# A threshold search over half the chip's counting work: VectorE compares without a running sum and TensorE adds the pieces

## The chip, the cores and the metric

The kernel runs on one core of one Trainium2 chip. The metric is the device time of one execution in microseconds (us), smaller is better. The core has five engines that run side by side and meet only at semaphores: TensorE (PE in the profile, with its weight loads as PEld), VectorE (DVE), ScalarE (ACT), GpSimd (POOL) and SyncE (SP), which issues the transfers.

## What is computed

Two hybrid layers over x of shape (2, 512, 512): attention, gated feed-forward and a state-space scan in the first, grouped attention, LoRA experts and a sparse gated feed-forward in the second. The change touches only the sparse one (`_L1_attn_b_ref`), which zeroes, in every row, the half of the 1376 gate values that is smallest in magnitude:

```python
s = jax.nn.silu(jnp.einsum('bsh,ih->bsi', x, w_gate))
B, S, I = s.shape                       # I = 1376
k = int(K_FACTOR * I)                   # 688
_, idx = jax.lax.top_k(-jnp.abs(s), k)
flat = flat.at[rows, idx.reshape(B * S, k)].set(0.0)
s = s * jnp.einsum('bsh,ih->bsi', x, w_up)
return jnp.einsum('bsi,hi->bsh', s, w_down)
```

## The kernel before

Each batch b (0 and 1) has 512 rows, held as four tiles t of 128 rows; so |s| is eight tiles `k_abs[b][t]` of 128 partitions x 1376 floats. The order of the stages is a list made by `schedule()`; each engine walks it in program order. The stage of interest is `("topk", 1)`, near the end. Before it stand the gate projections, behind it two normalisations and two LoRA stages.

The threshold of each row is found by a search over the 31 bits of a positive float (`K_BITS`). In step n each batch has a candidate per row (`k_cand`, integer bits, read as a float). For every row the number of values under the candidate is counted; from the count the bit is kept or cleared and the next one set. The counting is shared out by `K_DVE = [1, 2]`:

- VectorE (`count_low`, L1798) takes tile 0 of batch 0 and tiles 0 and 1 of batch 1: one instruction compares 1376 values with the row's candidate and also sums the ones into `k_cnt` (`accum_out`).
- ScalarE (L1367) takes the other five tiles: a Sign activation of candidate minus value, summed into `k_diff`.

`update(b, n)` on VectorE turns counts into the next candidate: L1805 (VectorE's tiles), L1807 (ScalarE's tiles, behind the semaphore `count[b]`), L1808 (the new bits, which signals `cand[b]`, for which both engines wait before they count that batch again). The order on VectorE is written out by hand, per step n: `count_low(0, n)`, `update(1, n-1)`, `count_low(1, n)`, `multiply_up(n-2)` in 24 of the 31 steps, `update(0, n)`. So the update of one batch lies behind a compare of the other. ScalarE alternates: batch 0's tiles, then batch 1's.

`multiply_up` (L1816) multiplies one result of the "up" projection, from a PSUM bank, into `k_s`. There are 24 such results: three column groups (512, 512, 352 wide) times eight row tiles; TensorE makes each with 12 matmuls (`mm3` is three matmuls: low x high, high x low, high x high). In the kernel before TensorE makes them at the start of the stage as fast as PSUM banks come free, one bank for each row tile, eight in all. The weights of the projection are units that SP loads and GpSimd splits into a high and a low part (L583, L584), in a ring of eight; a unit is split when TensorE has released the one eight before it.

After the search `threshold(b)` counts once more, on VectorE with L1827, the tiles that ScalarE had (three of batch 0, two of batch 1), adjusts their thresholds, and eight `mask` steps follow, then the down projection.

Of the kernel before, what the change touches and what calls it, by code (L numbers as in the profile page):

```python
# [49 lines left out]
K_DVE = [1, 2]  # L50
# [187 lines left out]
k_bits k_cand_0 k_cand_1 k_less_0 k_less_1 k_count_0 k_count_1 k_thr k_diff k_mask k_gate k_up k_silu k_up_kept k_abs k_masked k_turned k_hi k_lo k_acc  # L238
# [16 lines left out]
def hybrid_layers(nc, x_d, units_d, const_d, small_d, bdown_d, out_d):  # L255
# [9 lines left out]
    with ExitStack() as ctx:  # L265
        def sb(name, shape, dt=F32):
            return ctx.enter_context(nc.sbuf_tensor(name, shape, dt))
# [7 lines left out]
        cand, less, count = ([s[f"k_{n}_{b}"] for b in range(B)] for n in ("cand", "less", "count"))  # L275
# [8 lines left out]
        ra_lo = sb("ra_lo", [P, HC * EW], F32R)  # L284
        negA = sb("negA", [P, DT * N_ST])
# [9 lines left out]
        sd = sb("sd", [P, TT])  # L295
        f_hi = sb("f_hi", [P, 2, 512], F32R)
        f_lo = sb("f_lo", [P, 2, 512], F32R)
# [75 lines left out]
        k_junk = k_eq.bitcast(BF16).rearrange("p (a c) -> p a c", a=2)  # L373
        k_sign = k_rank.bitcast(BF16).rearrange("p (a c) -> p a c", a=2)
# [249 lines left out]
        def _(pe):  # L624
# [40 lines left out]
            def release(k=1):  # L665
                at["u"] += k
                at["owed"] += k
# [382 lines left out]
            def topk(_):  # L1050
                for j, w in enumerate(TK_W):
                    for b in range(B):
                        for t in range(TT):
                            rows(claim(b * TT + t, s["k_up_kept"]), [("tu", j, k) for k in range(HC)], hT_hi[:, b], hT_lo[:, b], t, w, s["k_up"], b)
# [341 lines left out]
        def _(dve):  # L1396
# [392 lines left out]
            def topk(_):  # L1789

                def count_low(b, n):

                    dve.wait_ge(cand[b], n + 1)
                    for t in range(K_DVE[b]):
                        last = before(n, b, t, 2)
                        if last:
                            dve.wait_ge(less[last[0]], last[1])
# [12 lines left out]

                def multiply_up(n):

                    j, b, t = n // (B * TT), n // TT % B, n % TT
                    y = k_s[b][t][:, 512 * j:512 * j + TK_W[j]]
                    need(s["k_up"])
                    go(V.tensor_tensor(y, ps[:, b * TT + t, 0:TK_W[j]], y, ALU.mult), s["k_up_kept"])  # L1816

                def threshold(b):
# [3 lines left out]
                    k_low, k_high, k_up = (k_late[:, n, 0:TT - m] for n in range(3))  # L1822
                    dve.wait_ge(cand[b], K_BITS + 1)
                    for r in range(B):
                        dve.wait_ge(less[r], K_DVE[r] * K_BITS)
# [3 lines left out]
                    go(V.tensor_scalar(k_low, late, 0xFFFF, None, ALU.bitwise_and))  # L1829
                    did(V.tensor_scalar(k_high, late, 16, None, ALU.logical_shift_right))  # L1830
                    did(V.tensor_tensor(k_low, k_low, k_up, ALU.add))
                    did(V.tensor_scalar(k_up, k_low, 16, None, ALU.logical_shift_right))
                    go(V.tensor_scalar(k_low, k_low, 0xFFFF, None, ALU.bitwise_and))
                    did(V.tensor_tensor(k_high, k_high, k_up, ALU.add))
                    did(V.tensor_scalar(k_high, k_high, 16, None, ALU.logical_shift_left))
                    did(V.tensor_tensor(late, k_high, k_low, ALU.bitwise_or), s["k_thr"])
# [35 lines left out]
                before = counted(lambda b: range(K_DVE[b]))  # L1872
# [129 lines left out]
```

## Time and profile before

| | us |
|---|---|
| median of 3 runs | 2974.18 |
| lowest and highest run | 2952.24 and 2975.89 |
| the profiled execution, its own time | 2963.2 |
| its span, first to last instruction | 2961.4 |
| busy: TensorE / VectorE / ScalarE / GpSimd | 2392.7 / 2051.9 / 1586.4 / 1214.4 |
| TensorE's granted clock, mean of the span | 0.898 of full speed |

The profile is of one execution. The busy times are sums over stages with different limits, so none of them says what bounds the threshold search; that has to be read from the stretch in which it runs, the last eighth of the span or so.

### The profile page before, as it was taken

The numbers are of one execution on the slowest core, as the hardware profiler recorded it, in microseconds if no ns is written. First come the engines' busy times: TensorE is split into PE (matmuls) and PEld (weight loads), VectorE is DVE, ScalarE is ACT, GpSimd is POOL, SyncE is SP. The second block draws the span as 40 slices with busy tenths as digits, with TensorE's granted clock in tenths as the row PEclk, the third lists the DMA queues.
The fourth block names the chain that finished last, engine by engine and source line by source line (L and its number), as shares of the span: only waits on it lengthen the run. The fifth ranks groups of instructions, "written<-read, shape, count | busy, mean of one in ns | idle before, by whom it ended". The sixth has DMA issues, their size and how long they took to land.

```text
span 2961.4 us, 36619 instructions
## 1 busy us (share of the span) xinstructions
PE 2392.7 (81%) x12216; PEld 1868.2 (63%) x12216; DVE 2051.9 (69%) x3145; ACT 1586.4 (54%) x3315; POOL 1214.4 (41%) x1016
## 2 busy tenths in 40 slices
PE   6986989858888848878899799998799998951068
PEld 4344347657777647777777588876688877741056
DVE  3743743668899657989753678874778874598984
ACT  2551641267876237787411466663566663799611
POOL 3022036253334422244465556673556663510081
PEclk9797799979999968999999899999999999965578
DMA  6224213020101120020123111121111121200011
GB/s 215 44 77 117 44 53 90 25 79 19 61 26 29 43 79 15 11 72 26 40 89 89 40 47 45 53 58 47 43 43 54 43 61 46 83 15 0 0 43 36
DMA packets 87842, 155.73 MB, mean 53 GB/s; under 512 B 8840, under 2 KB 17672, under 8 KB 87528
## 3 DMA queue, kind: packets, MB, share of 16 engines
q1 hardware_dynamic: 87656, 153.38, 17.6%
q8 instruction: 100, 1.64, 0.2%
q14 instruction: 86, 0.70, 0.1%
HBM read 138.21 MB, written 14.75 MB: 52 GB/s over the span
## 4 chain that ended last, share of the span: by engine, by line
PE 46%; DVE 18%; ACT 15%; issue 8%; POOL 3%; DVEq 0%; ACTq 0%; POOLq 0%
PE ps L640 40%; ACT tables L1367 5%; PE ps L654 5%; DVE m L1580 2%; DVE m L1606 2%; DVE f_lo L1406 2%; ACT m L1231 2%; DVE m_front L1527 1%; PE ps L779 1%; POOL w_lo L584 1%; ACT m L1210 1%; DVE f_hi L1405 1%; DVE loose L1509 1%; ACT L1231 1%; ACT tables L1200 1%
## 5 line engine op out<-in xcount | busy, mean ns | idle before, releaser
L583 POOL TENSOR_SCALAR w_hi<-w_in 128x512 fp32r<-128x512 f32 x430 | 352.0, 819 | 1219.5 <-PE ps L640 663.9
L584 POOL TENSOR_TENSOR w_lo<-w_in,w_hi 128x512 fp32r<-128x512 f32 x430 | 648.0, 1507 | 35.9
L640 PE MATMUL ps<-hT_hi,w_lo 128*128 128x512 f32 x864 | 364.0, 421 | 29.4 <-DVE a L1451 12.7
L640 PE MATMUL ps<-hT_lo,w_hi 128*128 128x512 f32 x864 | 346.1, 401 | 0.0
L640 PE MATMUL ps<-hT_hi,w_hi 128*128 128x512 f32 x864 | 345.6, 400 | 0.0
L1606 DVE TENSOR_TENSOR_SCAN m<-m,m 128x1028 f32<-128x1028 f32 x128 | 315.1, 2462 | 10.3 <-ACT m L1231 3.1
L640 PEld LDWEIGHTS ps<-m,tables 128*128 128x128 f32 x2048 | 253.3, 196 | 53.6 <-ACT tables L1200 25.6
L640 PE MATMUL ps<-m,tables 128*128 128x128 f32 x2048 | 258.3, 280 | 32.7 <-ACT tables L1200 32.6
L654 PE MATMUL ps<-tables,m 128*128 128x128 f32 x1024 | 144.3, 284 | 100.2 <-DVE m L1606 72.2
L1231 ACT ACTIVATE m<-m_rows,negA 128x256 f32<-128x256 f32 x512 | 217.7, 504 | 0.4
L1200 ACT ACTIVATE tables<-ps 128x512 f32<-128x512 f32 x256 | 139.1, 593 | 142.9 <-PE ps L654 142.9
L640 PEld LDWEIGHTS ps<-hT_hi,w_lo 128*128 128x128 f32 x864 | 168.5, 195 | 65.5 <-DVE a L1451 16.1
L640 PE MATMUL ps<-g,g 128*128 128x128 f32 (+3 forms) x704 | 173.2, 394 | 38.4 <-ACT g L1292 15.2
L640 PEld LDWEIGHTS ps<-hT_hi,w_hi 128*128 128x128 f32 x864 | 167.7, 194 | 38.4
L1580 DVE TENSOR_TENSOR m<-m,m 128x1024 f32<-128x1024 f32 x128 | 187.4, 1464 | 5.9 <-ACT m L1192 3.9
L654 PEld LDWEIGHTS ps<-tables,m 128*128 128x128 f32 x1024 | 117.8, 145 | 116.0 <-issue 84.7
L640 PEld LDWEIGHTS ps<-hT_lo,w_hi 128*128 128x128 f32 x864 | 168.8, 195 | 29.9
L640 PEld LDWEIGHTS ps<-g,g 128*128 128x128 f32 x704 | 121.2, 192 | 100.3 <-issue 61.5
L640 PE MATMUL ps<-w_hi,g 128*128 128x512 f32 x512 | 177.3, 407 | 7.5 <-DVE x_sb L1409 4.7
L1479 DVE TENSOR_REDUCE a<-ps 128x2 f32<-128x1024 f32 x128 | 150.1, 1221 | 44.7 <-PE ps L640 44.3
L1133 ACT ACTIVATE a<-ps 128x512 f32<-128x512 f32 x256 | 138.9, 595 | 72.6 <-PE ps L640 72.2
L640 PE MATMUL ps<-a,a 48*128 48x512 f32 (+1 forms) x512 | 147.7, 529 | 30.9 <-ACT a L1133 17.8
(247 smaller groups left out, 5314.0 us busy)
## 6 DMA issues: line engine op xcount, KB each, us to landing
w_in<-units SPq DMA_DIRECT2D x430, 256.0 KB, 2.6
stack_scratch<-a SPq DMA_DIRECT2D x48, 256.0 KB
a<-stack_scratch SPq DMA_DIRECT2D x64, 192.0 KB, 4.5
m<-bc_scratch SPq DMA_DIRECT2D x16, 512.0 KB, 5.4
out<-x_sb SPq DMA_DIRECT2D x2, 1024.0 KB, 4.3
tables<-small SPq DMA_DIRECT2D x1, 1143.0 KB, 10.3
x_sb<-x SPq DMA_DIRECT2D x4, 256.0 KB, 3.5
x_sb<-x SPq DMA_DIRECT2D x1, 1024.0 KB, 7.9
```

The lines of the kernel that those rows point to most:

```text
L583: c["did"](nc.gpsimd.tensor_scalar(w_hi[:, r], raw, 1.0, 1.0, ALU.mult, ALU.mult), s["unit_hi"])
L584: c["did"](nc.gpsimd.tensor_tensor(w_lo[:, r], raw, w_hi[:, r].bitcast(F32), ALU.subtract), s["unit_split"])
L640: ins = T.matmul(out, lhsT, rhs, start=start, stop=stop)
L654: ins = T.transpose(out, in_, ident)
L1133: go(A(a_pT[:, kT % 2 * 4 + pair * 2 + h], ps[:, 4 + h], ACT.Exp, scale=A_DK ** -0.5), s["a_exp"])
L1200: go(A(m_hT[:, part], ps[:, 6 - part], ACT.Copy), s["m_hT_kept"])
L1231: go(A(m_dA[:, n % DA_RING * NG + r, 1:SEG], m_dt[:, tile % 4], ACT.Exp, scale=negA[:, st:st + 1]), s["m_dA"])
L1367: A(k_sign[:, done % 2], k_abs[b][t], ACT.Sign, bias=k_cand[:, b].bitcast(F32)[:, t:t + 1], scale=-1.0, accum_out=k_diff[:, b, t:t + 1]).t ...
L1406: did(V.tensor_tensor(lo, src, hi.bitcast(F32), ALU.subtract), sem)
L1479: go(V.reduce_max(top, ps[:, pair * 2:pair * 2 + 2], AX.X), s["a_max"])
L1580: go(V.tensor_tensor(m_st[:, slot:slot + NG, 1:SEG], m_dtx[:, i % 2].unsqueeze(1).broadcast_to([P, NG, HL]), m_bc[:, g * NG:(g + 1) * NG], ...
L1606: V.tensor_tensor_scan(states, m_dA[:, dA:dA + NG].rearrange("p a t -> p (a t)"), states, 0.0, ALU.mult, ALU.add)\
```

## The change

`K_DVE` becomes `[2, 2]`: VectorE has four tiles and ScalarE four. VectorE's compare has no `accum_out` any more: it writes 0.5 or -0.5 per value (is-less, then minus 0.5) in bf16 into buffers of its own, `k_low[b][t]`. TensorE then adds eight pieces of 172 columns of each such tile onto one another, in PSUM, by multiplying with a bf16 identity matrix (`k_ident`): 8 matmuls per tile, 32 per step. VectorE's update begins with a reduction over the remaining 172 columns of both tiles (128x344 in PSUM, two sums out), behind a new semaphore `total[b]`, and then has one comparison for all four tiles in place of two.

TensorE's order is now written out: per step `sums(0, n)`, the first half (6 matmuls) of up result n, `sums(1, n)`, its second half. The up results go round six PSUM banks (`K_BANKS`); banks 6 and 7 take the sums. `threshold(b)` has two tiles to count for each batch.

```diff
-K_DVE = [1, 2]
+K_DVE = [2, 2]
+K_CHUNK = INTER // 8
+K_BANKS = 6
 ...
+                def sums(b, n):
+                    o = claim(K_BANKS + b, summed[b])
+                    if b == n == 0:
+                        need(s["k_ident_set"])
+                    for t in range(K_DVE[b]):
+                        pe.wait_ge(less[b], K_DVE[b] * n + t + 1)
+                        for r in range(INTER // K_CHUNK):
+                            ins = T.matmul(o[:, t * K_CHUNK:(t + 1) * K_CHUNK], k_ident, k_low[b][t][:, r * K_CHUNK:(r + 1) * K_CHUNK],
+                                           start=r == 0, stop=(r + 1) * K_CHUNK == INTER)
+                    ins.then_inc(total[b], 1)
+
+                for n in range(K_BITS):
                     for b in range(B):
-                        for t in range(TT):
-                            rows(claim(b * TT + t, s["k_up_kept"]), ...)
-                    release(HC)
+                        sums(b, n)
+                        if n < B * TT * len(TK_W):
+                            up(n, b)
 ...
                     for t in range(K_DVE[b]):
-                        V.tensor_scalar(k_junk[:, (n + b + t) % 2], k_abs[b][t], k_cand[:, b].bitcast(F32)[:, t:t + 1], None, ALU.is_lt, ALU.add,
-                                        accum_out=k_cnt[:, b, t:t + 1]).then_inc(less[b], 1)
+                        V.tensor_scalar(k_low[b][t], k_abs[b][t], k_cand[:, b].bitcast(F32)[:, t:t + 1], 0.5, ALU.is_lt, ALU.subtract)\
+                            .then_inc(less[b], 1)
 
                 def update(b, n):
                     bit, m = float(1 << K_BITS - 1 - n), K_DVE[b]
-                    dve.wait_ge(less[b], m * (n + 1))
-                    go(V.tensor_scalar(k_no[:, b, 0:m], k_cnt[:, b, 0:m], TOPK - 0.5, bit, ALU.is_ge, ALU.mult))
+                    dve.wait_ge(total[b], n + 1)
+                    did(V.tensor_reduce(k_diff[:, b, 0:m], ps[:, K_BANKS + b, 0:m * K_CHUNK].rearrange("p (t c) -> p t c", t=m), AX.X, ALU.add), summed[b])
                     dve.wait_ge(count[b], (TT - m) * (n + 1))
-                    did(V.tensor_scalar(k_no[:, b, m:], k_diff[:, b, m:], 2.0 * TOPK - INTER - 0.5, bit, ALU.is_ge, ALU.mult))
+                    did(V.tensor_scalar(k_no[:, b], k_diff[:, b], -0.5, bit, ALU.is_ge, ALU.mult))
                     V.scalar_tensor_tensor(k_cand[:, b], k_cand[:, b], k_bit[:, n + 1:n + 2], k_no[:, b], ALU.bitwise_or, ALU.bitwise_xor)\
                         .then_inc(cand[b], 1)
```

`up(n, part)`, not shown, is the old `rows` for one result cut in two at its inner loop.

## Rows read from the trace of the kernel before

**Rows 1.** Windows view of the search: length, busy and count per engine, clock, DMA.
```profile
2553.00:2775.00 222.00, 86.15 (x284) 68.56 (x283) 198.68 (x398) 221.18 (x311) 22.85 (x24) 0.63 0.05 16
```
**Rows 2.** Chain of work that ended last, same stretch, by line.
```profile
by line: ACT tables L1367 65.8%; issue 33.0%; DVE tables L1827 1.5%; DVE k_rows L1808 0.1%; DVE k_rows L1807 0.1%; DVE k_rows L1871 0.0%; ACTq L1362 0.0%
```
**Rows 3.** ScalarE's count of one tile, all 31 steps: ns min/median/max, first and last start.
```profile
L1367 ACT ACTIVATE tables<-loose,k_rows x31: 1424/1426/1429, 2559.1 to 2773.0; 128x1376 bf16<-128x1376 f32 x31
```
**Rows 4.** Timeline of VectorE inside the search: start us, us, instruction, idle before.
```profile
2671.21 0.69 DVE L1816 TENSOR_TENSOR k<-ps,k 128x512 f32<-128x512 f32 x1
2671.81 0.14 DVE L1805 TENSOR_SCALAR k_rows<-k_rows 128x1 int32<-128x1 f32 x1
...
2674.74 0.17 DVE L1807 TENSOR_SCALAR k_rows<-k_rows 128x2 int32<-128x2 f32 x1 [0.65 <-ACT tables L1367]
2674.95 0.22 DVE L1808 SCALAR_TENSOR_TENSOR k_rows<-k_rows,k_rows,k_rows 128x4 int32<-128x4 int32 x1
2675.20 1.65 DVE L1798 TENSOR_SCALAR_CACHE_REDUCE tables<-k,k_rows 128x1376 bf16<-128x1376 f32 x1
...
2676.78 1.64 DVE L1798 TENSOR_SCALAR_CACHE_REDUCE tables<-k,k_rows 128x1376 bf16<-128x1376 f32 x1
...
2685.47 0.52 DVE L1816 TENSOR_TENSOR k<-ps,k 128x352 f32<-128x352 f32 x1
2685.91 0.14 DVE L1805 TENSOR_SCALAR k_rows<-k_rows 128x1 int32<-128x1 f32 x1
```
**Rows 5.** Single lines of VectorE, whole run: ns min/median/max, starts, forms.
```profile
L1798 DVE TENSOR_SCALAR_CACHE_REDUCE tables<-k,k_rows x93: 1640/1645/1649, 2553.3 to 2769.4; 128x1376 bf16<-128x1376 f32 x93
L1550 DVE TENSOR_SCALAR tables<-m_rows x16: 427/430/1387, 611.0 to 1383.5; 128x512 f32<-128x512 f32 x16
L1466 DVE TENSOR_SCALAR negA<-negA x1: 228/228/228, 72.4 to 72.4; 128x128 f32<-128x128 f32 x1
L1429 DVE TENSOR_SCALAR n<-x_sb,mv,sd x64: 536/545/1543, 8.5 to 2933.6; 128x512 f32<-128x512 f32 x64
L1669 DVE TENSOR_REDUCE g<-ps x192: 424/558/683, 1664.8 to 2447.4; 128x1 f32<-128x256 f32 x64, 128x1 f32<-128x384 f32 x64, 128x1 f32<-128x512 f32 x64
```
**Rows 6.** Timeline of VectorE: four L1429, GpSimd idle, and four, GpSimd working.
```profile
2921.79 1.92 DVE L1429 TENSOR_SCALAR n<-x_sb,mv,sd 128x512 f32<-128x512 f32 x4
8.51 4.10 DVE L1429 TENSOR_SCALAR n<-x_sb,mv,sd 128x512 f32<-128x512 f32 x4
```
**Rows 7.** The new candidate's instruction, as in rows 5.
```profile
L1808 DVE SCALAR_TENSOR_TENSOR k_rows<-k_rows,k_rows,k_rows x62: 221/223/1323, 2559.3 to 2779.0; 128x4 int32<-128x4 int32 x62
```
**Rows 8.** Timeline of TensorE: 512, 128 and 136 moving columns at full clock.
```profile
1201.36 2.05 PE L640 MATMUL ps<-m,tables 128*128 128x128 f32 x16 [0.88 <-ACT tables L1200]
...
2559.18 0.39 PE L640 MATMUL ps<-w_hi,hT_hi 128*128 128x512 f32 x1
2559.41 0.39 PE L640 MATMUL ps<-w_hi,hT_lo 128*128 128x512 f32 x1
...
2927.35 0.42 PE L640 MATMUL ps<-ra_lo,hT_hi 128*128 128x136 f32 x1
2927.57 0.41 PE L640 MATMUL ps<-ra_hi,hT_hi 128*128 128x136 f32 x1
```
**Rows 9.** Page, costliest groups: busy us, mean ns of one, idle before, releaser.
```profile
L640 PE MATMUL ps<-m,tables 128*128 128x128 f32 x2048 | 258.3, 280 | 32.7 <-ACT tables L1200 32.6
```
**Rows 10.** Windows view, columns as in rows 1: a dense stretch, and two of the search.
```profile
1200.00:1240.00 40.00, 35.77 (x255) 31.95 (x254) 37.36 (x30) 33.81 (x77) 10.28 (x7) 1.00 0.00 1
2581.00:2630.00 49.00, 31.64 (x85) 22.03 (x84) 44.72 (x93) 49.00 (x69) 1.40 (x2) 0.75 0.04 11
2644.00:2686.00 42.00, 23.33 (x72) 20.61 (x72) 37.90 (x80) 42.00 (x60) 0.00 (x0) 0.50 0.00 0
```
**Rows 11.** Chain behind the search, in order of time: start us, us, line.
```profile
2772.11 1.67 DVE tables L1827 x2
2773.80 1.67 DVE tables L1827 x2
```

More of the change, by code:

```diff
@@ L274, in hybrid_layers @@
         max_in = [s["a_max_in_0"], s["a_max_in_1"]]
-        cand, less, count = ([s[f"k_{n}_{b}"] for b in range(B)] for n in ("cand", "less", "count"))
+        cand, less, count, total, summed = ([s[f"k_{n}_{b}"] for b in range(B)] for n in ("cand", "less", "count", "sum", "summed"))
         stack_out = [s["a_stack_out_0"], s["a_stack_out_1"]]
@@ L284, in hybrid_layers @@
         ra_lo = sb("ra_lo", [P, HC * EW], F32R)
+        negA_at = nc.sbuf_base
         negA = sb("negA", [P, DT * N_ST])
@@ L295, in hybrid_layers @@
         sd = sb("sd", [P, TT])
+        f_at = [nc.sbuf_base]
         f_hi = sb("f_hi", [P, 2, 512], F32R)
+        f_at.append(nc.sbuf_base)
         f_lo = sb("f_lo", [P, 2, 512], F32R)
@@ L373, in hybrid_layers @@
         k_junk = k_eq.bitcast(BF16).rearrange("p (a c) -> p a c", a=2)
+        k_ident = nc.alloc_sbuf_tensor_at("k_ident", [P, P], BF16, offset=negA_at, align_bytes=4)[:, :]
+        k_low = [[k_junk[:, 0], k_junk[:, 1]]]
+        k_low.append([nc.alloc_sbuf_tensor_at(f"k_low_{n}", [P, INTER], BF16, offset=base, align_bytes=4)[:, :] for n, base in enumerate(f_at)])
         k_sign = k_rank.bitcast(BF16).rearrange("p (a c) -> p a c", a=2)
@@ L1050, in topk, with up @@
             def topk(_):
-                for j, w in enumerate(TK_W):
+                def up(n, part):
+                    j, b, t = n // (B * TT), n // TT % B, n % TT
+                    o = claim(n % K_BANKS, s["k_up_kept"]) if part == 0 else ps[:, n % K_BANKS]
+                    w, rows_w = TK_W[j], slice(t * P, (t + 1) * P)
+                    for k in range(2 * part, 2 * part + 2):
+                        hi, lo = unit(("tu", j, k), k)
+                        mm3(o[:, 0:w], hT_hi[:, b, k, rows_w], hT_lo[:, b, k, rows_w], hi[:, 0:w], lo[:, 0:w],
+                            k == 0, k == HC - 1, s["k_up"] if k == HC - 1 else None)
+                    if part and n % (B * TT) == B * TT - 1:
+                        release(HC)
+                def sums(b, n):
[9 more added lines that the diff above has]
+                for n in range(K_BITS):
                     for b in range(B):
-                        for t in range(TT):
-                            rows(claim(b * TT + t, s["k_up_kept"]), [("tu", j, k) for k in range(HC)], hT_hi[:, b], hT_lo[:, b], t, w, s["k_up"], b)
-                    release(HC)
+                        sums(b, n)
+                        if n < B * TT * len(TK_W):
+                            up(n, b)
                 for b in range(B):
@@ L1815, in multiply_up @@
                     need(s["k_up"])
-                    go(V.tensor_tensor(y, ps[:, b * TT + t, 0:TK_W[j]], y, ALU.mult), s["k_up_kept"])
+                    go(V.tensor_tensor(y, ps[:, n % K_BANKS, 0:TK_W[j]], y, ALU.mult), s["k_up_kept"])
                 def threshold(b):
@@ L1821, in threshold @@
                     late, thr = c_b[:, m:], c_b.bitcast(F32)
-                    k_low, k_high, k_up = (k_late[:, n, 0:TT - m] for n in range(3))
+                    k_lower, k_high, k_up = (k_late[:, n, 0:TT - m] for n in range(3))
                     dve.wait_ge(cand[b], K_BITS + 1)
-                    for r in range(B):
-                        dve.wait_ge(less[r], K_DVE[r] * K_BITS)
                     for t in range(m, TT):
@@ L1828, in threshold @@
                     did(V.tensor_scalar(k_up, k_cnt[:, b, m:], TOPK - 0.5, None, ALU.is_lt))
-                    go(V.tensor_scalar(k_low, late, 0xFFFF, None, ALU.bitwise_and))
+                    go(V.tensor_scalar(k_lower, late, 0xFFFF, None, ALU.bitwise_and))
                     did(V.tensor_scalar(k_high, late, 16, None, ALU.logical_shift_right))
-                    did(V.tensor_tensor(k_low, k_low, k_up, ALU.add))
-                    did(V.tensor_scalar(k_up, k_low, 16, None, ALU.logical_shift_right))
-                    go(V.tensor_scalar(k_low, k_low, 0xFFFF, None, ALU.bitwise_and))
+                    did(V.tensor_tensor(k_lower, k_lower, k_up, ALU.add))
+                    did(V.tensor_scalar(k_up, k_lower, 16, None, ALU.logical_shift_right))
+                    go(V.tensor_scalar(k_lower, k_lower, 0xFFFF, None, ALU.bitwise_and))
                     did(V.tensor_tensor(k_high, k_high, k_up, ALU.add))
                     did(V.tensor_scalar(k_high, k_high, 16, None, ALU.logical_shift_left))
-                    did(V.tensor_tensor(late, k_high, k_low, ALU.bitwise_or), s["k_thr"])
+                    did(V.tensor_tensor(late, k_high, k_lower, ALU.bitwise_or), s["k_thr"])
                 def mask(b, t):
@@ L1871, in topk @@
                     V.memset(k_cand[:, b], 1 << K_BITS - 1).then_inc(cand[b], 1)
-                before = counted(lambda b: range(K_DVE[b]))
+                assert 2 * TOPK == INTER
+                go(V.tensor_copy(k_ident, ident), s["k_ident_set"])
                 for n in range(K_BITS):
```

5 lines of the change are left out of this document (1 added, 4 removed).

## The prediction, made before the changed kernel ran

> **What bounds the kernel now.** I read the page first: TensorE is busiest over the span, which says nothing of this change. So I took the windows view of the search alone [rows 1]: in 222 us ScalarE is busy 221.18, VectorE 198.68, TensorE 86.15, GpSimd 22.85. The chain of that stretch names ScalarE's count for 65.8% and "issue" for most of the rest [rows 2]; "issue" there is ScalarE going from one activation to the next, as its busy time shows. The single line [rows 3] gives the step: one tile's activation started at 2559.1 in the first step and at 2773.0 in the last, (2773.0 - 2559.1)/30 = 7.13 us for five tiles, 1.426 each. VectorE waits for ScalarE 0.65 us at the update [rows 4]. So the search is ScalarE's five tiles, 31 times, and VectorE is not far behind. It runs from the first compare at 2553.3 [rows 5] to the start of the threshold count at 2772.1 [rows 11]: 218.8 us. That stretch is what the change can shorten; the rest of the program stays as it is.
>
> **ScalarE.** Four tiles a step: 4 x 1.426 = 5.70 us. If nothing else bound the search it would end after 31 x 5.70 = 177 us. So the gain has a ceiling near 42 us, and the question is what comes next.
>
> **VectorE's compare.** No row has this instruction: 1376 floats in, bf16 out, one operand per row, no sum. Below: the instructions of this kind without a sum take 228 ns for 128 columns and 430 for 512 (L1466 and L1550, constants only [rows 5]), 0.526 ns a column, so 1376 columns cost 228 + 1248 x 0.526 = 884 ns. L1429, the same width with two per-row operands, takes 545, so one operand costs (545 - 430)/2 = 58 ns. Together 942 ns. Above: the summing form, 1645 ns (L1798 [rows 5]); VectorE's reductions cost 558 - 424 = 134 ns for 128 columns (L1669 [rows 5]), 1.05 ns a column, the same slope. I take 942: the instruction drops what sets L1798 apart, and the kind is that of the three rows; what differs is the bf16 output. Back to back the starts lie closer than the durations: four L1429 take 1.92 us [rows 6], (1.92 - 0.545)/3 = 0.458, which is 0.087 less than 0.545. So a compare takes 0.855 us of VectorE's time, four take 3.42. Three of the old ones took 3 x 1.57 (2675.20 to 2676.78 [rows 4]) = 4.71.
>
> One place where the Trainium skill and the rows part: its page VectorE: DVE Perf Modes, section The TRN2 errata, gives 58 cycles plus the columns over the speed-up, which for this compare is 777 ns, an estimate by that page. For 512 columns it would give 327 ns where the trace has 430, so the trace disagrees; by the page the sum below would be 31 x 4 x 0.165 = 20 us shorter until ScalarE binds.
>
> **VectorE's update.** Out goes L1805; in comes a reduction of 344 columns from PSUM. From 424 ns at 256 columns it is 424 + 88 x 1.05 = 516, plus 0.035 for its own semaphore (L1807 of 0.17 us to L1808 is 0.21 [rows 4]). Then 0.21 for the comparison and 0.25 for L1808 to the next compare [rows 4]. Together 1.015 us, twice a step: 2.03. `multiply_up` is unchanged, 0.60 for 512 columns and 0.44 for 352 (start to start [rows 4]). A step on VectorE is therefore 3.42 + 2.03 + 0.60 = 6.05 in 16 steps, 5.89 in 8, 5.45 in the 7 without a multiply. In 24 steps that is more than ScalarE's 5.70: VectorE becomes the bound, by little. In the last five steps ScalarE falls 0.25 a step behind, 1.25 us in all; `update(1, n)` asks for its count only 1.4 us after it is there, so VectorE still sets the pace. In the first step `update(1)` is missing, 1.0 less. Sum: 16 x 6.05 + 8 x 5.89 + 7 x 5.45 - 1.0 = 181.1 us.
>
> **TensorE's sums.** Per half step 16 small matmuls and, in 24 steps, 6 matmuls of an up result, 6 x 0.23 = 1.38 (2559.18 to 2559.41 [rows 8]). The nearest row for a small one is 128 columns: 16 in 2.05 us, a single one lasting 0.28 [rows 8, 9], so (2.05 - 0.28)/15 = 0.118 us, weights loaded each time. Below: the 512-column pace by width, 0.23 x 172/512 = 0.077. Above: the slow 136-column form, 0.22 [rows 8]. I take 0.10, between the 128-column row and the streaming pace, as the bf16 identity is half the bytes of the float one in that row. A half step is then 16 x 0.10 + 1.38 = 2.98, a step 5.96: hidden under 6.05. Nothing of it is on the path as long as that holds: `update(0)` needs `total[0]` 0.86 + 1.0 + 1.7 + 0.6 us, some 3.3, after the second compare ended, and the eight matmuls of that tile need 0.8 plus about 0.3 until seen. If the cover goes (0.118 each), TensorE's step is 2 x (1.89 + 1.38) = 6.54 and costs 0.49 in 16 steps, 8 us.
>
> The clock: with TensorE 89% busy with such small matmuls it was granted 1.00, 2.4 GHz; with bursts and waits it was granted 0.75 and later 0.50, 1.2 GHz [rows 10]. In the new loop it is nearly always busy for 24 steps, so I take 2.4 GHz there; in the last seven steps it may fall, where 32 sums at twice the price, 6.4 us, exceed 5.45. I book 3 us for that and for the start.
>
> **GpSimd.** The work that speaks against the change. It splits 12 units in the stretch, 24 instructions, 22.85 us [rows 1]. L1798 never takes over 1649 ns [rows 5], but the kinds without a sum are held: four L1429 take 4.10 us while GpSimd works and 1.92 when it doesn't [rows 6]; L1808 reaches 1323 for 223 [rows 7]. Until now VectorE's slack hid that; if the new compares are held like L1429, they are on the path. The loss was 2.18 of 4.10 us, 0.53; compares fill 3.42/6.05 = 0.57 of a step; 22.85 x 0.53 x 0.57 = 6.9, with the small instructions 8 us. Below: nothing. Above: all 22.85.
>
> The Trainium skill, page SBUF — State Buffer, section Who interferes with whom, says that of such a VectorE instruction and a GpSimd one the later blocks fully until the other ends. Read so, every one of the 24 would cost its whole duration, 22.85 us, and the gain would be 13 us. Of that the trace bears out about half [rows 6].
>
> **Threshold.** Batch 0 has two late tiles, not three: 1.69 us less [rows 11]. The two of batch 1 stay. The identity is copied once, 0.2 us.
>
> **Sum.** 181.1 + 3 + 8 = 192.1 against 218.8 is 26.7 less; with the threshold and the copy 28.2. TensorE's price is as likely over 0.10 as under, and only over costs, so I take off 2: 26 us. The profiled execution took 2963.2 (span 2961.4): 2937. The median of the runs is 11 above that execution, so against it 2948.
>
> **Rivals,** times against the median.
> - GpSimd and TensorE cost almost nothing: 218.8 - 181.1 + 1.5 = 39 less, 2935. For it: the units could fall into reductions and multiplies, which read PSUM. Against it: 0.57 of each step is compares.
> - TensorE binds mildly, 0.118 a matmul: 8 us given back, with GpSimd's full share 15 more: between 2956 and 2971. It decides from (6.05/2 - 1.38)/16 = 0.103 us a matmul.
> - TensorE binds hard: at 0.22 a half step is 3.52 + 1.38 = 4.90, a step 9.8; 16 x 3.75 + 8 x 3.1 (0.16 for a 352-column matmul, by width) + 7 x 1.6 = 96 more than the sum: 3044, slower. It decides where TensorE's step passes the 7.13 of today, 0.137 us a matmul. The clock at 1.2 GHz throughout would do the same. For it: in the search TensorE was mostly at 0.50. Against it: a bound TensorE never pauses, and dense stretches had 1.00 [rows 10].
> - The compare keeps the slope of the sum because its output is bf16: 1.57 a compare, 4 x 0.715 = 2.86 more a step, 31 x 2.86 = 89, less GpSimd's 8: 3029, slower. It decides at a compare of 0.855 + (7.13 - 6.05)/4 = 1.13 us. For it: no row has a bf16 output without a sum. Against it: three lines agree on the slope, and other lines with a changed kind of output (L1807, float to int32 [rows 4]) show no harm.
>
> **How the numbers follow.** The forecast (VectorE binds, GpSimd 3 to 15 us) 0.62, nearly nothing lost 0.12, TensorE mildly 0.11, TensorE hard 0.05, slow compare 0.10. About 1% (30 us) is what a measurement of this kernel can tell from no change. The forecast is 4 us short of that; with its spread and the runs' own (24 us between lowest and highest) 0.26 of its 0.62 lie beyond it. Faster 0.12 + 0.26 = 0.38, same 0.36 + 0.11 = 0.47, slower 0.15. The range leaves out the two slower cases and some edge: from the near-lossless case less some of the runs' scatter, 2930, to the mild TensorE case with all of GpSimd's price, 2972.
>
> **What the profile after would show.** The compare at 0.94 us and starts 0.86 apart; the step at 6.05 us while up results are made and about 5.5 behind them; ScalarE with gaps, its counts 1.43; VectorE's waits for TensorE near nothing; small matmuls 0.10 apart at clock 1.00; in the three stretches in which GpSimd splits, compares up to 2 us; from the first compare to the first L1827 some 192 us. I would be wrong if the reduction waited for TensorE step after step, or the compare took 1.6, or the compares lengthened outside GpSimd's work too.

## The result, and the profile after

| | before | after |
|---|---|---|
| median (lowest to highest), us | 2975.03 (2952.24 to 2989.08), 4 runs | 2938.74 (2937.88 to 2947.09), 4 runs |
| profiled execution, its own time | 2963.2 | 2938.07 |
| its span | 2961.4 | 2936.3 |
| from the first compare to the first threshold count | 218.8 | 193.0 |
| from there to the first mask | 12.1 | 10.9 |
| from the mask to the end | 177.2 | 180.1 |

The ratio is 0.989 with a 95% interval of 0.985 to 0.993. A second set of executions of the changed kernel gave 2941.67 us (2932.06 to 2952.25, 6 runs) against 2969.93, ratio 0.991 (0.988 to 0.994). So the change makes the kernel about 1% faster, and whether a little more or a little less than 1% these runs do not say. The two stretches that the change touches became 27.0 us shorter. The profiled execution as a whole became 25.1 us shorter, because the stretch from the mask to the end took 2.9 us more; a second execution of the same changed kernel took 173.7 us there (last section), so this row shows scatter and not the change.

The search of the changed kernel in the windows view (columns: window, length, busy time and count per engine, TensorE's granted clock, DMA), and the chain that ended last in it, by line:

```profile
2553.00:2745.00 192.00, 158.56 (x1274) 125.74 (x1275) 185.66 (x330) 177.40 (x245) 28.40 (x24) 0.94 0.07 19
...
by line: issue 24.9%; DVE k_low L1826 20.7%; DVE tables L1826 18.1%; DVE k_rows L1833 14.1%; DVE k_rows L1836 9.1%; DVE k L1844 6.8%; DVE k_rows L1835 6.3%; ACT loose L1385 0.3%; DVE k_rows L1897 0.0%; DVE k_ident L1899 0.0%; DVEq L443 0.0%
```

Beside [rows 1] and [rows 2]: ScalarE, which was busy for all but 0.8 us of 222, now has 14.6 us of 192 free; VectorE is busy 185.66 of 192; the chain is a list of VectorE's own lines, where 65.8% of it had been ScalarE's count. The bound has moved from ScalarE to VectorE, as forecast. TensorE went from 86 of 222 to 159 of 192 and does not appear in the chain.

The groups of the search (busy us, mean ns of one, idle time before them and its releaser):

```profile
L1398 ACT ACTIVATE tables<-k,k_rows 128x1376 bf16<-128x1376 f32 x62 | 88.8, 1433 | 8.7 <-DVE k_rows L1836 8.2 <-DVE k_rows L1897 0.3
L1826 DVE TENSOR_SCALAR k_low<-k,k_rows 128x1376 bf16<-128x1376 f32 x62 | 59.7, 1004 | 1.1
L1826 DVE TENSOR_SCALAR tables<-k,k_rows 128x1376 bf16<-128x1376 f32 x62 | 59.6, 1004 | 1.1
L1078 PE MATMUL ps<-tables,k_ident 128*128 128x172 bf16 x496 | 50.4, 250 | 23.3 <-DVE tables L1826 23.3
L1078 PE MATMUL ps<-k_low,k_ident 128*128 128x172 bf16 x496 | 48.5, 248 | 12.2 <-DVE k_low L1826 12.2
L1833 DVE TENSOR_REDUCE k_rows<-ps 128x2 f32<-128x344 f32 x61 | 30.9, 507 | 0.0
```

Who waits for whom is read in the last column. TensorE waits for VectorE's compares (23.3 and 12.2 us); VectorE never waits for TensorE: 0.0 before the reduction L1833. ScalarE waits for VectorE's new candidate (L1836).

One clean step on VectorE, with GpSimd idle (start us, us, instruction):

```profile
2590.98 1.78 DVE L1826 TENSOR_SCALAR tables<-k,k_rows 128x1376 bf16<-128x1376 f32 x2
2592.67 0.51 DVE L1833 TENSOR_REDUCE k_rows<-ps 128x2 f32<-128x344 f32 x1
2593.22 0.17 DVE L1835 TENSOR_SCALAR k_rows<-k_rows 128x4 int32<-128x4 f32 x1
2593.42 0.22 DVE L1836 SCALAR_TENSOR_TENSOR k_rows<-k_rows,k_rows,k_rows 128x4 int32<-128x4 int32 x1
2593.68 1.79 DVE L1826 TENSOR_SCALAR k_low<-k,k_rows 128x1376 bf16<-128x1376 f32 x2
2595.37 0.69 DVE L1844 TENSOR_TENSOR k<-ps,k 128x512 f32<-128x512 f32 x1
2595.97 0.51 DVE L1833 TENSOR_REDUCE k_rows<-ps 128x2 f32<-128x344 f32 x1
...
2596.98 1.78 DVE L1826 TENSOR_SCALAR tables<-k,k_rows 128x1376 bf16<-128x1376 f32 x2
```

2596.98 - 2590.98 = 6.00 us for the step. The instructions follow one another without a gap. Where GpSimd splits, the same lines look like this, VectorE first and then GpSimd:

```profile
2605.70 2.14 DVE L1826 TENSOR_SCALAR k_low<-k,k_rows 128x1376 bf16<-128x1376 f32 x2
2607.76 0.67 DVE L1844 TENSOR_TENSOR k<-ps,k 128x512 f32<-128x512 f32 x1
2608.36 0.50 DVE L1833 TENSOR_REDUCE k_rows<-ps 128x2 f32<-128x344 f32 x1
2608.89 0.17 DVE L1835 TENSOR_SCALAR k_rows<-k_rows 128x4 int32<-128x4 f32 x1
2609.09 0.59 DVE L1836 SCALAR_TENSOR_TENSOR k_rows<-k_rows,k_rows,k_rows 128x4 int32<-128x4 int32 x1
2609.72 2.04 DVE L1826 TENSOR_SCALAR tables<-k,k_rows 128x1376 bf16<-128x1376 f32 x1
```

```profile
2606.06 1.05 POOL L591 TENSOR_SCALAR w_hi<-w_in 128x512 fp32r<-128x512 f32 x1 [40.76 <-PE ps L648]
2607.19 1.78 POOL L592 TENSOR_TENSOR w_lo<-w_in,w_hi 128x512 fp32r<-128x512 f32 x1
2609.06 0.62 POOL L591 TENSOR_SCALAR w_hi<-w_in 128x512 fp32r<-128x512 f32 x1
2609.76 1.27 POOL L592 TENSOR_TENSOR w_lo<-w_in,w_hi 128x512 fp32r<-128x512 f32 x1
```

A compare that starts at 2609.72 takes 2.04 us instead of 0.93: GpSimd's L592 runs from 2609.76 for 1.27. The holding goes both ways. The L592 that meets compares takes 1.78 and not 1.27, and the 24 instructions are busy 28.40 us where they took 22.85 before [rows 1]. The single lines over the whole run (ns min/median/max):

```profile
L1826 DVE TENSOR_SCALAR tables<-k,k_rows x62: 928/935/2045, 2552.3 to 2740.8; 128x1376 bf16<-128x1376 f32 x62
L1833 DVE TENSOR_REDUCE k_rows<-ps x62: 496/508/517, 2555.7 to 2750.2; 128x2 f32<-128x344 f32 x62
L1835 DVE TENSOR_SCALAR k_rows<-k_rows x62: 169/170/701, 2556.2 to 2750.8; 128x4 int32<-128x4 f32 x62
L1836 DVE SCALAR_TENSOR_TENSOR k_rows<-k_rows,k_rows,k_rows x62: 221/223/1202, 2556.4 to 2751.0; 128x4 int32<-128x4 int32 x62
L1844 DVE TENSOR_TENSOR k<-ps,k x24: 516/680/689, 2571.4 to 2716.8; 128x512 f32<-128x512 f32 x16, 128x352 f32<-128x352 f32 x8
```

The compare and the two small instructions of the update are held (maximum far over median), the two lines that read PSUM, L1833 and L1844, are not. Two more groups of the search, as above, for the means of the small instructions:

```profile
L1836 DVE SCALAR_TENSOR_TENSOR k_rows<-k_rows,k_rows,k_rows 128x4 int32<-128x4 int32 x61 | 17.1, 281 | 2.1
L1835 DVE TENSOR_SCALAR k_rows<-k_rows 128x4 int32<-128x4 f32 x61 | 11.4, 187 | 2.1
```

The price in the search is mean less median, times count: 124 x (1004 - 935.5) ns = 8.5 us for the compares (their medians are 935 and 936 in the two buffers), 61 x (281 - 223) = 3.5 for L1836, 61 x (187 - 170) = 1.0 for L1835. Together 13.0 us.

Without that, steps of 6.00 us (512 columns multiplied), 5.84 (352) and 5.41 (none; 2718.28 to 2723.69) would give 16 x 6.00 + 8 x 5.84 + 7 x 5.41 - 1.0 = 179.6 us. Adding 13.0 gives 192.6, and the search took 193.0.

### The profile page after: what moved, and what is told of

It reads as the page before. It is cut to its first block, busy times and chain, and to the rows that moved or that the text cites. A ratio compares the mean times of both kernels' runs of the same rounds, so it can differ in the third digit from the quotient of the medians.

```text
span 2936.3 us, 38540 instructions
## 1 busy us (share of the span) xinstructions
PE 2463.9 (84%) x13208; PEld 1925.6 (66%) x13208; DVE 2041.0 (70%) x3082; ACT 1544.7 (53%) x3253; POOL 1215.5 (41%) x1016
## 4 chain that ended last, share of the span: by engine, by line
PE 48%; DVE 23%; ACT 9%; issue 8%; POOL 3%; DVEq 0%; ACTq 0%; POOLq 0%
PE ps L648 41%; PE ps L662 5%; DVE m L1611 2%; DVE m L1637 2%; DVE f_lo L1437 2%; ACT m L1262 2%; DVE k_low L1826 1%; PE ps L787 1%; DVE m_front L1558 1%; DVE tables L1826 1%; POOL w_lo L592 1%; DVE loose L1540 1%; DVE f_hi L1436 1%; DVE k_rows L1833 1%; ACT L1262 1%
## 5 line engine op out<-in xcount | busy, mean ns | idle before, releaser
L592 POOL TENSOR_TENSOR w_lo<-w_in,w_hi 128x512 fp32r<-128x512 f32 x430 | 643.7, 1497 | 35.9
L648 PE MATMUL ps<-w_hi,g 128*128 128x512 f32 x512 | 177.2, 407 | 7.5 <-DVE x_sb L1440 4.7
```

Of the source, the lines that this page charges most:

```text
L592: c["did"](nc.gpsimd.tensor_tensor(w_lo[:, r], raw, w_hi[:, r].bitcast(F32), ALU.subtract), s["unit_split"])
L648: ins = T.matmul(out, lhsT, rhs, start=start, stop=stop)
```

## The experiments

**The theory**: VectorE's own work bounds the search, and the 13 us between 179.6 and 193.0 are what GpSimd's splits take from it. The rivals: TensorE binds or nearly binds; the round of count, sum and new candidate binds, whoever does the work; the gain is in the balance of the tiles alone, or in the new way of summing alone. For each run the stretches were read from its trace as in the table above; they are compared among themselves, since they repeat far better than the whole time does.

### The balance alone

The kernel before, with four tiles on each engine and the summing compare (the second edit only picks the scratch buffer):

```diff
-K_DVE = [1, 2]
+K_DVE = [2, 2]
-V.tensor_scalar(k_junk[:, (n + b + t) % 2], k_abs[b][t], k_cand[:, b].bitcast(F32)[:, t:t + 1], None, ALU.is_lt, ALU.add,
+V.tensor_scalar(k_junk[:, t % 2], k_abs[b][t], k_cand[:, b].bitcast(F32)[:, t:t + 1], None, ALU.is_lt, ALU.add,
```

> The kernel before with K_DVE = [2, 2] alone: four tiles on VectorE, still compared with the running sum, four on ScalarE; TensorE adds nothing. My theory (the saving comes from the compare without a sum, the new split alone costs): a step on VectorE is 4 x 1.57 + 2 x 0.53 + 0.60 = 7.94 us with a 512-column multiply, 7.78 with 352, 7.34 without; from the first compare to the first threshold count some 240 us against 218.8 before, about 21 us slower in all than before. Rival (moving ScalarE's fifth tile away is what pays): 31 x 5.70, some 180 us, 38 us faster than before.

Measured: 2997.28 us (2984.51 to 3001.87) against 2972.04, ratio 1.0075 (1.0046 to 1.0104); search 243.5 us. One step of its VectorE, by its first and its last line:

```profile
2661.42 1.65 DVE L1798 TENSOR_SCALAR_CACHE_REDUCE tables<-k,k_rows 128x1376 bf16<-128x1376 f32 x1
...
2669.35 1.65 DVE L1798 TENSOR_SCALAR_CACHE_REDUCE tables<-k,k_rows 128x1376 bf16<-128x1376 f32 x1
```

2669.35 - 2661.42 = 7.93 us a step with a 512-column multiply, and ScalarE waits for L1808 in it. The fourth tile is worth nothing to a VectorE that sums as it compares; it makes the kernel 0.75% slower. The balance needs the cheap compare.

### The sums alone

The changed kernel with three tiles on VectorE and five on ScalarE:

```diff
-K_DVE = [2, 2]
+K_DVE = [1, 2]
```

> The changed kernel with K_DVE = [1, 2]: the compare without a sum and the adding on TensorE, but three tiles on VectorE and five on ScalarE as before. My theory: ScalarE binds with 5 x 1.426 = 7.13 us a step, so the search stays 218.8 us (within 2), and the whole is within 3 us of before. Rival (the cheaper compare pays by itself): the search gets shorter by up to 31 x 0.7 = 22 us.

Measured: 2974.51 us (2962.96 to 2981.59), ratio 0.9988 (0.9966 to 1.0011); search 220.5 us. VectorE waits for ScalarE's count again:

```profile
2702.95 0.17 DVE L1835 TENSOR_SCALAR k_rows<-k_rows 128x4 int32<-128x4 f32 x1 [0.84 <-ACT tables L1398]
...
2707.23 0.17 DVE L1835 TENSOR_SCALAR k_rows<-k_rows 128x4 int32<-128x4 f32 x1 [1.36 <-ACT tables L1398]
```

So the cheap compare and TensorE's sums alone change nothing either: ScalarE's five tiles still set the step. The gain is a product of the two parts: the one makes VectorE's fourth tile affordable, the other hands it over.

### GpSimd kept quiet

```diff
+quiet = first_unit[[it[0] for it in items].index("topk")] + HC
...
+w = 2 if u >= quiet and u < quiet + 12 else 512
-c["did"](nc.gpsimd.tensor_scalar(w_hi[:, r], raw, 1.0, 1.0, ALU.mult, ALU.mult), s["unit_hi"])
+c["did"](nc.gpsimd.tensor_scalar(w_hi[:, r, 0:w], raw[:, 0:w], 1.0, 1.0, ALU.mult, ALU.mult), s["unit_hi"])
...
```

> The changed kernel, but GpSimd splits only 2 of 512 columns of the 12 weight units that it splits during the search, so that its 24 instructions there are short; the rest of these units holds what was there before, so the up projection and the first part of the down projection are computed from wrong weights. My theory: the search of the changed kernel, 193.0 us, holds 13 us in which VectorE is held up by GpSimd; most of that goes, 181 to 184 us. Rival (the 13 us are waits for TensorE or its clock): still 191 to 194.

Measured: 2934.53 us (2930.66 to 2938.59), ratio 0.985 (0.9808 to 0.9892); search 180.3 us, 12.7 less than in the changed kernel and 0.7 above the bare sum of 179.6. The compares:

```profile
L1829 DVE TENSOR_SCALAR tables<-k,k_rows x62: 923/932/943, 2557.8 to 2733.5; 128x1376 bf16<-128x1376 f32 x62
L1829 DVE TENSOR_SCALAR k_low<-k,k_rows x62: 928/932/940, 2559.5 to 2736.3; 128x1376 bf16<-128x1376 f32 x62
```

The maximum fell from 2045 ns to 943. It is GpSimd's splitting that lengthens them, and the 13 us are its price: shown, not only argued.

### TensorE with less to do

```diff
-mm3(o[:, 0:w], hT_hi[:, b, k, rows_w], hT_lo[:, b, k, rows_w], hi[:, 0:w], lo[:, 0:w],
-    k == 0, k == HC - 1, s["k_up"] if k == HC - 1 else None)
+mm(o[:, 0:w], hT_hi[:, b, k, rows_w], hi[:, 0:w],
+   k == 0, k == HC - 1, s["k_up"] if k == HC - 1 else None)
```

> The changed kernel, but each up result is made by 4 matmuls instead of 12 (only high x high), so the low parts are left out of the up projection. My theory: TensorE is off the path; the search stays 193.0 us, within 1. Rival (TensorE's half steps hold the updates back): the search gets shorter by more than 3 us.

Measured: 2944.55 us (2937.93 to 2957.8), ratio 0.9889 (0.984 to 0.9939); search 192.9 us, against 193.0. TensorE's busy time in the search fell from 158.6 to 127.6 us and nothing came of it. TensorE is off the path.

### Pieces half as wide, and a quarter

If TensorE is off the path, how far is it from it? The width of the pieces shifts work from VectorE's reduction to TensorE: half the width is twice the matmuls.

```diff
-K_CHUNK = INTER // 8
+K_CHUNK = INTER // 16
```

> The changed kernel with pieces half as wide: 16 pieces of 86 columns, so 32 small matmuls of 172 columns per half step in place of 16 of 344/2, and a reduction of 172 columns in place of 344. It asks where TensorE becomes the bound. Theory (at 0.085 us a small matmul, read in the changed kernel, less if a matmul's price falls with its width): the reduction costs VectorE 172 x 1.05 ns = 0.18 us less, twice a step; TensorE's half step is between 32 x 0.06 + 1.38 = 3.30 and 32 x 0.085 + 1.38 = 4.10 us, a step of 6.6 to 8.2 us in the 24 steps with up results, against VectorE's 5.64. Then the search is 0.6 to 2.2 us a step longer than 193.0 in 24 steps and about as long in the other seven: 205 to 246 us, VectorE waiting at its reduction for TensorE in every half step. Rival (TensorE has room left, the matmuls follow at half the price): the search shortens by 31 x 0.36 = 11 us to 182 us, and no wait stands before the reduction.

Measured: 2937.19 us (2932.1 to 2956.74), ratio 0.99 (0.9864 to 0.9937), and in a second set 2940.36, ratio 0.9917 (0.9888 to 0.9947); search 186.1 us both times. The theory of this run was wrong about TensorE. Its timeline at full clock (the idle time before the group and its releaser in brackets), one full half step, then two groups without up results between them, one at full clock and a slower one, where the window of 2720 to 2740 us was granted 0.67:

```profile
2638.67 1.58 PE L1078 MATMUL ps<-tables,k_ident 128*128 128x86 bf16 x32
...
2709.88 1.57 PE L1078 MATMUL ps<-tables,k_ident 128*128 128x86 bf16 x32 [1.38 <-DVE tables L1826]
...
2734.93 2.45 PE L1078 MATMUL ps<-k_low,k_ident 128*128 128x86 bf16 x32 [0.40 <-DVE k_low L1826]
```

32 matmuls in 1.57 us are 0.05 apart, and in the changed kernel 16 of twice the width take 1.53 (shown further down): the price goes with the width, and a weight load before every one sets no floor at this width. The search didn't lose, and it gained 6.9 us rather than the rival's 11. VectorE's step is now 6.00 - 0.36 = 5.64 (2637.58 to 2643.24 in its timeline is 5.66), just under ScalarE's 5.70. In the last five steps, whose VectorE work is 5.41 - 0.36 = 5.05 us, ScalarE sets the pace: the half steps of the trace are 2.85 apart, 5.70 a step. That gives back 5 x 0.65 = 3.3 of the rival's 11 us.

A quarter of the width asks the same once more, with 64 matmuls a half step:

```diff
-K_CHUNK = INTER // 8
+K_CHUNK = INTER // 32
```

> The changed kernel with pieces a quarter as wide: 32 pieces of 43 columns, 64 small matmuls of 86 columns... that is, of 43 columns for each of two tiles, per half step, and a reduction of 86 columns. In the kernel with pieces of 86 columns 32 small matmuls took 1.57 us, 0.047 apart, half of the 0.085 of the 172-column... of the wide ones. Theory A (the price goes on falling with the width, 0.025 at 43 columns): TensorE's half step is 64 x 0.025 + 1.38 = 2.98 us, the step 5.96 against ScalarE's 5.70, so the search is 186.1 plus at most 24 x 0.26 = 6, 186 to 193 us. Theory B (the weight load before each matmul is the floor, near 0.045): the half step is 64 x 0.045 + 1.38 = 4.26, the step 8.5, and the search 186 + 24 x 2.8 = 253 us, with VectorE waiting for TensorE at its reduction in every half step: TensorE binds hard, as in the rival of the prediction.

Measured: 2938.71 us (2921.16 to 2956.79), ratio 0.9902 (0.9872 to 0.9932); search 188.5 us, inside what theory A named and 65 us from theory B. TensorE's timeline:

```profile
2649.14 1.77 PE L1078 MATMUL ps<-tables,k_ident 128*128 128x43 bf16 x64
2652.23 1.78 PE L1078 MATMUL ps<-k_low,k_ident 128*128 128x43 bf16 x64
```

64 in 1.78 us are 0.028 apart: even there the price still falls with the width, if no longer in proportion. The two groups start 3.09 us apart, so TensorE needs 6.18 us a step with a 512-column up result, more than VectorE's own work of 5.47. Here TensorE binds: where the up results are 512 wide, VectorE comes to wait for it at one reduction in each step, and the steps become 6.18 us long. One of these waits, on VectorE:

```profile
2627.80 0.25 DVE L1833 TENSOR_REDUCE k_rows<-ps 128x2 f32<-128x86 f32 x1 [0.57 <-PE ps L1078]
```

There are eight such waits, 3.7 us in all, and the search is 2.4 us longer than with pieces of 86 columns. In the last steps ScalarE's 5.70 us is the bound in both, so narrower pieces have nothing left to win.

### VectorE without the multiplication

```diff
-go(V.tensor_tensor(y, ps[:, n % K_BANKS, 0:TK_W[j]], y, ALU.mult), s["k_up_kept"])
+go(V.tensor_tensor(y[:, 0:2], ps[:, n % K_BANKS, 0:2], y[:, 0:2], ALU.mult), s["k_up_kept"])
```

> The changed kernel with the multiplication of the up results done on 2 of the 512 or 352 columns (it leaves the other columns of that product out), so that VectorE has 0.5 us less to do in 24 steps. Theory (VectorE's step is 6.00 us and ScalarE's 5.70 lies just under it, so ScalarE takes over as the bound): the step falls to 5.70 in 24 steps, not to 5.5; with what GpSimd holds still there in part, the search is 184 to 188 us, ScalarE without gaps. Rival (VectorE alone binds, ScalarE never): 24 x 0.53 = 13 us less, 180 us. Rival (the bound is the round of count, sum and threshold, not VectorE's work): 193 us.

Measured: search 183.8 us, 9.2 less; the whole 2940.3 us, ratio 0.9899 (0.9871 to 0.9926), which does not show it (the profiled execution entered its search at 2574.1 us, against 2552.3 in the changed kernel's). VectorE's step without the product, 2637.35 to 2642.83 in its timeline, is 5.48 us, and ScalarE runs through it without a gap:

```profile
2638.79 1.43 ACT L1398 ACTIVATE tables<-k,k_rows 128x1376 bf16<-128x1376 f32 x1
...
2643.07 1.43 ACT L1398 ACTIVATE tables<-k,k_rows 128x1376 bf16<-128x1376 f32 x1
```

2643.07 - 2638.79 is 4.28 us for three tiles, 1.426 each, the pace of [rows 3]. So VectorE's work is the bound and not the round as such (which would have left 193). The theory of this run was wrong in one point: it had the 24 steps at ScalarE's 5.70, and they took 5.48 where the product had 512 columns and 5.47 where it had 352. That is 16 x 0.52 + 8 x 0.37 = 11.3 us less. ScalarE had waited for VectorE where GpSimd splits (0.91 us at 2637.35) and so could fall behind by 0.2 us a step for a while without holding anything up; that this is the reason was not tried by itself. Only in the last five steps, 5.70 us each, does VectorE wait for ScalarE's count, 1.3 us in all. The other 0.8 us between 11.3 and 9.2 fit the small instructions beside GpSimd: L1835 costs 2.0 us more than in the changed kernel (mean 220 ns for 187) and L1836 1.1 less (263 for 281). For this split of the tiles ScalarE's four counts, 31 x 5.70 = 177 us, stay the floor.

### GpSimd's work moved and narrowed

```diff
+w = TK_W[order[u][1]] if order[u][0] == "tu" else 512
+if order[u] == ("td", 0) and not held:
+    held.append(u)
+    pool.wait_ge(s["k_cand_0"], K_BITS + 1)
-c["did"](nc.gpsimd.tensor_scalar(w_hi[:, r], raw, 1.0, 1.0, ALU.mult, ALU.mult), s["unit_hi"])
+c["did"](nc.gpsimd.tensor_scalar(w_hi[:, r, 0:w], raw[:, 0:w], 1.0, 1.0, ALU.mult, ALU.mult), s["unit_hi"])
...
```

> The changed kernel with GpSimd's splits for the next products moved: it splits only the columns of each unit that are used (352 of 512 in a third of the units of the up weights), and the units of the down weights only once the search of batch 0 has ended, so that they don't run beside VectorE's compares. All results are computed. Theory (GpSimd's work during the search costs VectorE 13 us, share by share): of the 24 instructions 8 leave the search and 5 become a third shorter, so 0.3 to 0.45 of 13 us comes back: search 187 to 189 us, and 4 to 6 us off the whole if the down products still find their units ready. Rival (the down products wait for the late units): the search is as short, but the time behind the first mask grows by some 5 us and the whole is unchanged.

Measured: search 187.4 us, 5.6 less than the changed kernel, as expected. But the stretch to the first mask went from 10.9 to 14.3 us, which neither theory had, and the whole shows no gain: 2942.07 us (2935.45 to 2970.2), ratio 0.9918 (0.9888 to 0.9948), beside 0.991 for the changed kernel. The place, on VectorE and on GpSimd:

```profile
2748.53 1.65 DVE L1857 TENSOR_SCALAR_CACHE_REDUCE tables<-k,k_rows 128x1376 bf16<-128x1376 f32 x1
...
2750.22 0.82 DVE L1858 TENSOR_SCALAR k_rows<-k_rows 128x2 int32<-128x2 f32 x1
...
2751.15 0.59 DVE L1860 TENSOR_SCALAR k_rows<-k_rows 128x2 int32<-128x2 int32 x1
...
2751.97 1.12 DVE L1862 TENSOR_SCALAR k_rows<-k_rows 128x2 int32<-128x2 int32 x1
```

```profile
2749.75 1.26 POOL L596 TENSOR_TENSOR w_lo<-w_in,w_hi 128x512 fp32r<-128x512 f32 x1
...
2751.80 1.26 POOL L596 TENSOR_TENSOR w_lo<-w_in,w_hi 128x512 fp32r<-128x512 f32 x1
```

The count (L1857) keeps its 1.65 us beside GpSimd, as L1798 did. But the chain of small integer instructions behind it does not: L1862 takes 1.12 us for 0.17, because it starts in the middle of an L596 and ends with it (2751.80 + 1.26 = 2753.06). Five of nine small instructions paid, 3.4 us in all. An instruction of 0.17 us that is held pays the rest of the GpSimd instruction that it meets, so of the work tried here a chain of small ones is the worst neighbour for it.

### Narrow pieces and better placed GpSimd work together

The last two ideas in one, with the late units two and two, so that each pair falls on the counts and not on what follows them:

```diff
-K_CHUNK = INTER // 8
+K_CHUNK = INTER // 16
+w = TK_W[order[u][1]] if order[u][0] == "tu" else 512
+if order[u][0] == "td" and len(held) < 3:
+    held.append(u)
+    if len(held) != 2:
+        pool.wait_ge(s["k_cand_%d" % (len(held) // 2)], K_BITS + 1)
...
```

> The changed kernel with pieces of 86 columns, GpSimd's splits cut to the used columns, and the four units of the down weights that fell into the search split later: two behind the end of the search of batch 0, two behind that of batch 1, each pair beside the counts of the thresholds. All results are computed. Theory (VectorE's work falls by 0.36 us a step, ScalarE's 5.70 binds, and what GpSimd takes from VectorE in the search is cut by 0.43 as before): 31 x 5.70 = 177, plus 0.57 of the 9.4 us that GpSimd still cost with pieces of 86: search 181 to 183 us; the threshold stretch loses 1 to 2 us rather than 3.4. Together some 10 us less than the changed kernel. Rival (what ScalarE loses to the late updates doesn't shrink with GpSimd's work): search 186 us.

Measured: 2926.51 us (2922.57 to 2938.57, 6 runs) against 2966.07, ratio 0.9879 (0.985 to 0.9907); search 180.2 us, to the first mask 11.9. Together 192.1 us against 203.9 in the changed kernel, 11.8 less. Of GpSimd's price 16 instructions are left in the search, and the chain behind each pair of counts pays 0.65 us once (L1859 takes 0.82 us for 0.17). By its stretches this is the best version of the study. By whole times it beats the kernel before clearly; against the version with narrow pieces alone, in the same set, the intervals still overlap (0.985 to 0.9907 and 0.9888 to 0.9947).

## Why the prediction was right, step by step

**VectorE becomes the bound: right.** The compare, for which no row existed, was put at 942 ns and 0.855 us from one start to the next; it measured 935, and two take 1.78, so their starts are 1.78 - 0.935 = 0.85 apart. The reading that carried the forecast was the slope over three lines of the same kind plus the price of a per-row operand. The bf16 output costs nothing over that sum, which closes the rival of 3029 us. The row that the prediction took from the Trainium skill (VectorE: DVE Perf Modes, The TRN2 errata) made it 777 ns; the trace disagrees, at 935. The same section says that this row under-predicts and puts the measured fixed term at about 150 cycles instead of 58, which the prediction passed over. With 150 the estimate is 873 ns here and 423 ns for the 512 columns that took 430 [rows 5]; with the 58 ns of a per-row operand it would be 931.

**The update, the step: right.** 1.015 us forecast; 2595.97 to 2596.98 is 1.01. The step came at 6.00, 5.84 and 5.41 us for 6.05, 5.89 and 5.45. Over 31 steps that is 179.6 for 181.1 us.

**TensorE hidden: right, with more room than forecast.** The timeline of the changed kernel, a group at full clock with the up matmul behind it, and a group of the last steps:

```profile
2592.06 1.53 PE L1078 MATMUL ps<-tables,k_ident 128*128 128x172 bf16 x16 [0.35 <-DVE tables L1826]
2593.38 0.48 PE L648 MATMUL ps<-w_hi,hT_lo 128*128 128x512 f32 x1
...
2740.99 2.45 PE L1078 MATMUL ps<-tables,k_ident 128*128 128x172 bf16 x16 [1.17 <-DVE tables L1826]
```

A single one lasts 0.25 us (the group's mean), so at full clock 16 are (1.53 - 0.25)/15 = 0.085 apart, where 0.10 was taken between bounds of 0.077 and 0.22, and 0.103 was where it would begin to bind. The value lies near the low bound, which went by width; the runs with pieces of 86 and 43 columns show that the price goes down with the width. The step taken in the prediction, from the row of 128 float columns [rows 8], was too careful.

**The clock: mis-sized by 3 us, to no cost.** In the stretches of the search with up results the granted clock was 0.95 to 1.00, and less behind them:

```profile
2615.00:2655.00 40.00, 36.13 (x284) 27.69 (x284) 38.70 (x71) 37.60 (x52) 1.16 (x1) 1.00 0.05 14
...
2700.00:2745.00 45.00, 31.45 (x272) 25.92 (x270) 43.28 (x85) 44.89 (x63) 0.00 (x0) 0.84 0.00 1
```

With TensorE busy for 36.13 of 40 us the granted clock was 1.00, 2.4 GHz. In the last steps, where TensorE pauses for up to 1.18 us before a group, the mean was 0.84: some groups of 16 still took 1.53 us and others 2.45, the pace of 1.2 GHz (the clock was 0.50 from 2745 to 2752 us). At the slow pace two groups, 4.9 us, are still under the step's 5.41. The prediction had taken twice the full-clock price, 6.4 us, from a small matmul of 0.10 that is 0.085. So the 3 us booked were not spent.

**GpSimd: the mechanism right, the term too small.** 8 us were booked between bounds of 0 and 22.85, and 13.0 were paid. The working was 22.85 x 0.53 x 0.57 = 6.9 for the compares and 1.1 for the small instructions. Measured were 8.5 and 4.5. Two things were missing: GpSimd's own instructions are lengthened too, so it works 28.40 us and not 22.85 (with that the same formula gives 8.6); and the small instructions L1835 and L1836 are held out of proportion to their length, 4.5 us, as the variant with moved splits shows again at the threshold. The rule of the Trainium skill (SBUF — State Buffer, Who interferes with whom), by which the later instruction waits for all of the other, was read by the prediction as a price of 22.85 us. For single pairs the trace bears the rule out (L1862 in the variant with moved splits ends with the L596 that it met). The sum, 13.0 of 28.40 us, needn't go against it, for the same section exempts reductions, VectorE instructions with at most one SBUF input outside the two-port modes, and the form that writes out its accumulator, and it lets either engine be the one that waits. The trace agrees on each: L1833 and L1844, which read PSUM, and the summing counts (1.65 us beside GpSimd) aren't held, and GpSimd's own instructions grew from 22.85 to 28.40 us. The 8 us booked, which went by [rows 6] and not by the page, were the nearer figure.

**The threshold: 1.69 forecast, 1.25 measured** (12.1 less 10.9 in the rounded table). The forecast counted the tile that is dropped and forgot that `update(1)` of the last step, with its new reduction, lies in the same stretch.

**The sum.** 179.6 + 0 + 13.4 = 193.0 in place of 181.1 + 3 + 8 = 192.1. The total is right within 1 us; in it 3 us too much for the clock and 1.5 too much for the steps stand against 5 too little for GpSimd. The 2 us taken off as an allowance for TensorE weren't needed either, and the threshold gave 0.4 less than booked. So the stretches gave 27.0 us where 26 were forecast, by errors that cancel. That is a piece of luck, and the term to remember is GpSimd's. Of the profiled execution the prediction said 2937; it took 2938.07, and that closeness holds some luck too, since the parts that the change doesn't touch came out 1.9 us longer.

**Where the forecast missed: the median.** 2948 was 2937 plus the 11 us by which the median of three runs lay over the profiled execution. The median of the changed kernel is 2938.74, on its own profiled execution and 9 us under the forecast. The step "against the median add 11" took an offset of one draw for a property of the kernel. In four sets of this study the kernel before has medians of 2975.03, 2972.04, 2969.93 and 2966.07, while its profiled execution took 2963.2: with the last of these the offset would be 3 us. That also decided the chances. The 0.62 given to the forecast was split at a line of 1% that lay 4 us from it, which made "no change that can be told" the likeliest outcome (0.47, against 0.38 for faster). The result lies 1.1% under the kernel before, so just past that line; its interval of 0.985 to 0.993 rules out that nothing changed, but doesn't rule out a gain smaller than 1%.

## What to carry to other kernels

When two engines share a loop, moving a tile pays only if the receiving engine's own price per tile falls first; neither half of such a change shows anything alone. Once an engine becomes the bound, look at who holds it: here a neighbour's work that had been free for a VectorE with slack took 13 us from a VectorE without it, a third of the possible gain of 39, and part of it came back by cutting unused columns and moving the work beside instructions that are not held. And size a sum over many small matmuls by the columns that they stream before assuming a fixed price for each.

## What was not expected

**Small bf16 matmuls still get cheaper with width down to 43 columns**, each with its weight load: 0.085 us apart at 172 columns, 0.05 at 86 and 0.028 at 43, so half the width costs somewhat more than half.

**The same code ahead of the search takes up to 30 us more or less.** The first compare began at 2552.3 us in the changed kernel's profiled execution, at 2559.1 in its second, and at 2582.4 in that of the version with pieces of 43 columns, whose program is the same up to there. The first 300 us of the changed kernel and of that version, by windows:

```profile
0.00:300.00 300.00, 222.76 (x992) 122.55 (x992) 147.00 (x202) 107.53 (x200) 53.58 (x60) 0.87 0.39 112
```

```profile
0.00:300.00 300.00, 234.77 (x923) 123.61 (x924) 128.19 (x182) 100.80 (x186) 53.85 (x60) 0.76 0.39 112
```

TensorE was granted 0.87 in one and 0.76 in the other. At the end of the program it is likewise: in the changed kernel's last stretch TensorE was granted 0.50 from 2912 to 2922 us, in its second execution 1.00 from 2906 to 2936, and from the mask to the end they took 180.1 and 173.7 us. What makes the clock fall in one execution and not in the next was not tried and stays open. With such scatter the intervals of whole times here reach 0.3 to 0.5% to either side, while the search, read from the trace, came out within 0.5 us for both kernels that were run twice (193.0 and 193.3; 186.1 and 186.1).
